# The order inside a group of expert matmuls: gate and up in turn, token tiles in turn

## The reference, cut to what matters

```
x = x + xattn(ctx, layernorm(x))          # scores, top 76 of each row, sigmoid, symmetrised
z = layernorm(x)
scores  = softmax(z @ gate_w.T);  weights, idx = top_k(scores, 2)
h   = einsum('td,eid->eti', z, w1)        # gate half, 128 hidden units per expert
g   = silu(h) * einsum('td,eid->eti', z, w3)   # times the up half
eo  = einsum('eti,edi->etd', g, w2)       # second projection
y   = sum over experts of eo * its weight (0 where not chosen)
out = x + y + shared expert of z (ws1, ws3, ws2)
```

## Time and profile before

| | before |
|---|---|
| median of 3 runs | 122.41 us |
| profiled execution | 122.40 us |
| its span | 120.6 us |
| TensorE busy (matmuls) | 105.2 us, 87% |
| VectorE busy | 83.1 us, 69% |
| GpSimd busy | 84.3 us, 70% |
| ScalarE busy | 55.0 us, 46% |
| mean granted TensorE clock | 0.929 of full speed |

### The profile page before, as it was taken

One profiled execution on the slowest core, in us unless ns is written; L12 is line 12 of the kernel. 1 busy time (PEld: TensorE's weight loads), 2 busy tenths in 40 slices (PEclk: granted clock), 3 DMA queues, 4 the chain that ended last, 5 costly groups with the idle time before them and its releaser, 6 DMA issues.

```text
span 120.6 us, 2390 instructions
## 1 busy us (share of the span) xinstructions
PE 105.2 (87%) x790; PEld 101.4 (84%) x790; DVE 83.1 (69%) x265; ACT 55.0 (46%) x128; POOL 84.3 (70%) x137
## 2 busy tenths in 40 slices
PE   6996082259999999999999999999989999999991
PEld 6775072158899989999999999999979999999990
DVE  6578996984695998769939896965555770708632
ACT  4149989299708612361768412104093243224310
POOL 4037878895799988999998899962827675075800
PEclk9999855555899999999999999999999999999999
DMA  2899992000000017000045000020441100902002
GB/s 55 206 297 297 323 369 79 0 5 3 0 5 0 0 44 313 0 3 0 0 130 226 0 0 0 8 90 0 163 185 43 49 0 3 345 8 90 0 0 87
DMA packets 7069, 10.32 MB, mean 86 GB/s; under 512 B 1360, under 2 KB 5968, under 8 KB 6544
## 3 DMA queue, kind: packets, MB, share of 16 engines
q1 hardware_dynamic: 6688, 10.13, 24.9%
q10 hardware_dynamic: 368, 0.04, 0.2%
HBM read 9.09 MB, written 1.08 MB: 84 GB/s over the span
## 4 chain that ended last, share of the span: by engine, by line
PE 75%; DVE 8%; ACT 5%; POOL 4%; issue 3%; DMA 2%; DVEq 1%; ACTq 0%; POOLq 0%; SPq 0%
PE ps_h L1248 21%; PE ps_u L1248 20%; PE ps_y L1276 16%; PE ps_u L1141 4%; PE ps_a L1276 3%; PE ps_c L1216 3%; PE ps_a L1176 2%; DMA weights<-gates 2%; PE ps_b L1199 2%; PE ps_h L1165 1%; DVE left L849 1%; POOL gc L423 1%; DVE near L855 1%; ACT qkT L551 1%; DVE g_lo L1001 1%
## 5 line engine op out<-in xcount | busy, mean ns | idle before, releaser
L423 POOL TENSOR_TENSOR gc<-prod,weights 128x512 f32<-128x512 f32 x16 | 25.5, 1609 | 13.3 <-DMA weights<-gates 7.4
L634 ACT ACTIVATE sil<-ps_h 128x512 f32<-128x512 f32 (+1 forms) x20 | 10.8, 549 | 25.1 <-PE ps_h L1248 24.8
L1001 DVE TENSOR_TENSOR g_lo<-gc,g_hi 128x512 fp32r<-128x512 f32 x16 | 13.3, 841 | 11.4 <-ACT g_hi L645 11.2
L1276 PE MATMUL ps_y<-dn_hi,g_hi 128*128 128x256 f32 x63 | 18.2, 289 | 0.5 <-DVE g_lo L1001 0.5
L1276 PE MATMUL ps_y<-dn_lo,g_hi 128*128 128x256 f32 x63 | 17.8, 282 | 0.0
L1276 PE MATMUL ps_y<-dn_hi,g_lo 128*128 128x256 f32 x63 | 17.8, 282 | 0.0
L645 ACT ACTIVATE g_hi<-gc 128x512 fp32r<-128x512 f32 x16 | 9.7, 625 | 13.8 <-POOL gc L423 13.8
L1248 PE MATMUL ps_h<-z_hi,up_hi 128*128 128x256 f32 x72 | 15.0, 289 | 0.3 <-issue 0.3
L1248 PE MATMUL ps_h<-z_lo,up_hi 128*128 128x256 f32 x72 | 14.5, 282 | 0.0
L1248 PE MATMUL ps_h<-z_hi,up_lo 128*128 128x256 f32 x72 | 14.4, 281 | 0.0
L1248 PE MATMUL ps_u<-z_hi,up_hi 128*128 128x256 f32 x72 | 14.4, 281 | 0.0
(11 more groups left out here) (173 smaller groups left out, 253.0 us busy)
## 6 DMA issues: line engine op xcount, KB each, us to landing
weights<-gates SPq DMA_DIRECT2D x4, 1024.0 KB, 4.5
x_sb<-in_x SPq DMA_DIRECT2D x4, 256.0 KB, 5.9
up_raw<-in_w1t SPq DMA_DIRECT2D x4, 256.0 KB, 6.4
up_raw<-in_w3t SPq DMA_DIRECT2D x4, 256.0 KB, 6.6
dn_raw<-in_w2t SPq DMA_DIRECT2D x4, 256.0 KB, 7.2
out_x<-fin SPq DMA_DIRECT2D x3, 256.0 KB, 2.4
out_x<-fin SPq DMA_DIRECT2D x2, 128.0 KB, 1.7
ctx_sb<-in_ctxT SPq DMA_DIRECT2D x1, 192.0 KB, 4.4
```

Of the source, the lines that this page charges most:

```text
L423: nc.gpsimd.tensor_tensor(gc[k % 2][:, :].rearrange("p (n t q) -> p n t q", n=2, t=T), prod[s][:, :].rearrange("p (n t q) -> p n t q", n=2 ...
L634: nc.scalar.activation(sil[i % 2][:, :w], ps_h[i % 2][:, :w], ACT.Silu).then_inc(silu_ready, 1)
L1001: nc.vector.tensor_tensor(g_lo[s][:, :], src[:, :], g_hi[s][:, :].bitcast(F32), ALU.subtract).then_inc(glo0_ready if s == 0 else glo_ready, 1)
L1276: last = nc.tensor.matmul(dst[:, t * D:(t + 1) * D], g[s][:, tok], w[:, e, :], start=(s == 0 and first and m == 0), stop=(s == SLOTS - 1 a ...
```

## The change

Two loops are written in another order. In the first projection the loop over the halves (a: gate, up) was the outermost; now it is the innermost, so a gate matmul into `ps_h` and an up matmul into `ps_u` alternate, both with the same moving operand. In the second projection the loop over the two token tiles moves inside the one over the three products; `down_last` keeps its order. `h_ready` is given by the last gate matmul and `u_ready` by the last up matmul, as before, and these are now the last two of the group. The waits for converted weights are for both halves at the start of a batch 0 group. The numbers of instructions are the same.

```
-                for a, (bank, ready) in enumerate(((ps_h, h_ready), (ps_u, u_ready))):
-                    for n, e in enumerate(experts_of(s)):
-                        dst = bank[i % 2][:, n * N:(n + 1) * N]
-                        m = 0
-                        for w, zz in ((up_hi, z_hi), (up_lo, z_hi), (up_hi, z_lo)):
-                            if b == 0 and n == 0 and m == 0:
-                                pe.wait_ge(up_hi_ready, 2 * s + a + 1)
-                            if b == 0 and n == 0 and w is up_lo:
-                                pe.wait_ge(up_lo_ready, 2 * s + a + 1)
-                            if zz is z_lo and a == 0 and n == 0:
-                                pe.wait_ge(zlo_ready, b + 1)
-                            for k in range(KD):
-                                last = nc.tensor.matmul(dst, w[:, e, a, k, :], zz[b % 2][:, k, :], ...)
-                                m += 1
-                    last.then_inc(ready, 1)
+                for n, e in enumerate(experts_of(s)):
+                    m = 0
+                    for w, zz in ((up_hi, z_hi), (up_lo, z_hi), (up_hi, z_lo)):
+                        if b == 0 and n == 0 and m == 0:
+                            pe.wait_ge(up_hi_ready, 2 * s + 2)
+                        if b == 0 and n == 0 and w is up_lo:
+                            pe.wait_ge(up_lo_ready, 2 * s + 2)
+                        if zz is z_lo and n == 0:
+                            pe.wait_ge(zlo_ready, b + 1)
+                        for k in range(KD):
+                            for a, bank in enumerate((ps_h, ps_u)):
+                                last = nc.tensor.matmul(bank[i % 2][:, n * N:(n + 1) * N], w[:, e, a, k, :],
+                                                        zz[b % 2][:, k, :], start=(m == 0), stop=(m == 3 * KD - 1))
+                                if m == 3 * KD - 1 and n == len(experts_of(s)) - 1:
+                                    last.then_inc((h_ready, u_ready)[a], 1)
+                            m += 1
...
             def down(b, s):
                 down_wait(b, s)
                 for n, e in enumerate(experts_of(s)):
-                    for t in range(T):
-                        last = down_tile(b, s, n, e, t)
+                    for m in range(3):
+                        for t in range(T):
+                            last = down_part(b, s, n, e, t, m)
                 last.then_inc(down_done, 1)
```

More of the change, by code:

```diff
@@ L1235, in up @@
                     pe.wait_ge(prod_ready, i - 1)
-                for a, (bank, ready) in enumerate(((ps_h, h_ready), (ps_u, u_ready))):
-                    for n, e in enumerate(experts_of(s)):
-                        dst = bank[i % 2][:, n * N:(n + 1) * N]
-                        m = 0
-                        for w, zz in ((up_hi, z_hi), (up_lo, z_hi), (up_hi, z_lo)):
-                            if b == 0 and n == 0 and m == 0:
-                                pe.wait_ge(up_hi_ready, 2 * s + a + 1)
-                            if b == 0 and n == 0 and w is up_lo:
-                                pe.wait_ge(up_lo_ready, 2 * s + a + 1)
-                            if zz is z_lo and a == 0 and n == 0:
-                                pe.wait_ge(zlo_ready, b + 1)
-                            for k in range(KD):
-                                last = nc.tensor.matmul(dst, w[:, e, a, k, :], zz[b % 2][:, k, :],
-                                                        start=(m == 0), stop=(m == 3 * KD - 1))
-                                m += 1
-                    last.then_inc(ready, 1)
+                for n, e in enumerate(experts_of(s)):
[14 more added lines that the diff above has]
+                            m += 1
             def down_wait(b, s):
@@ L1268, in down_wait, with down_part @@
                     pe.wait_ge(glo_ready, gated(b, s))
-            def down_tile(b, s, n, e, t):
+            def down_part(b, s, n, e, t, m):
+                g, w = ((g_hi, dn_hi), (g_hi, dn_lo), (g_lo, dn_hi))[m]
                 tok = slice(n * N + t * P, n * N + (t + 1) * P)
[L1273 to L1279, removed]
+                dst = ps_a if b == LAST and t == 1 else ps_y
+                first = t == 0 or b == LAST
+                return nc.tensor.matmul(dst[:, t * D:(t + 1) * D], g[s][:, tok], w[:, e, :],
+                                        start=(s == 0 and first and m == 0),
+                                        stop=(s == SLOTS - 1 and n == 1 and m == 2), skip_group_check=True)
             def down(b, s):
@@ L1291, in down_last @@
                     for n, e in enumerate(experts_of(SLOTS - 1)):
-                        last = down_tile(LAST, SLOTS - 1, n, e, t)
+                        for m in range(3):
+                            last = down_part(LAST, SLOTS - 1, n, e, t, m)
                     last.then_inc(last_tile, 1)
```

## The result

The changed kernel took 123.04 us as the median of 4 runs (122.80 to 123.64), the kernel before 122.03 us beside it (4 runs, 121.19 to 122.43). The ratio is 1.0124, with a 95% interval of 1.0071 to 1.0176: slower. The ratio is worked out from the single runs and is not the quotient of the two medians, which differ by 1.01 us, or 0.8%. The ratios in this document leave out executions in a slower state, two of the twelve of the second projection alone and two of the kernel before. The forecast was 123.5 us, with a range of 122.3 to 125.2.

A forecast was written before the change was run, and what follows sets the result against it. From about 31 us TensorE bounds the kernel, through its matmul count, step and waits. The terms 1.30 - 0.15 - 0.27 + 0.25 = +1.13 us on 122.40 us gave 123.5 us, range 122.3 to 125.2 us.

The forecast's parts named there:

- The step: Distance between matmuls in both projections: claimed unchanged at 0.118 to 0.120 us, term 0, bounds plus and minus 5 ns.
- the step rivals: Alternation shortens the distance between matmuls (5 ns: 120.3 us, chance 0.09) or lengthens it (5 ns: 126.8 us, chance 0.10).
- The wait for z: TensorE's transposes of batch 1's z wait behind the later silu of batch 0, slot 1: +1.30 us, down to 1.0.
- The wait for z_lo: Very first group, third product: wanted four matmuls later, so its weight load's wait shrinks: -0.15 us, between 0 and -0.19.
- The old wait at (0,3): Batch 0, slot 3, at 43.18 us: TensorE's wait for slot 1's product vanishes: -0.27 us, 0 the other end.
- The products that follow: VectorE's products come about 0.48 us later, behind silu; TensorE waits at batch 1, slot 3: +0.25 us, between 0 and 0.5.
- The remaining slots have more room: Slots after batch 1, slot 3: no added wait; the wait at 89.70 us moves as a whole.
- the tail: Last slot's g_lo and its matmuls: 0.83 us of slack against 0.48, so 0, at most 0.1 us.
- hidden after all: Rival: something after 38 us swallows the stall; with z in time, only 0.25 us left, 122.0 to 122.9 us; chance 0.13.
- The clock did not fall in the new wait: Rival: TensorE's clock falls in the new idle stretch around the transposes, 2.7 us lost, 126.2 us; chance 0.04.

The follow-up runs named there:

- the second projection alone: Only the second projection alternates its token tiles, first projection as in the kernel before; ratio to the kernel before 0.9995.
- the kernel with `ps_u` first: The kernel before with the halves swapped, all of ps_u filled and then all of ps_h, no alternation; ratio to the kernel before 1.0175.
- the first projection alone: Only the first projection alternates gate and up, second projection as in the kernel before; median 123.12 us, ratio to the kernel before 1.0128.
- z and product moved ahead: Changed kernel with batch 1's normalisation ahead of the silu of batch 0, slot 1, and that slot's product ahead of routing; ratio to the kernel before 1.0034.
- all but (0,1): The changed kernel, but with the gate and up group of batch 0, slot 1 in the old order; ratio to the kernel before 1.0062.
- z ahead: The changed kernel with batch 1's normalisation moved ahead of the silu of batch 0, slot 1 on ScalarE; median 122.82 us, ratio to the kernel before 1.0101.
- the two swaps and no alternation: Kernel before with batch 1's normalisation ahead of the silu of batch 0, slot 1, and that slot's product ahead of routing; ratio to the kernel before 0.9981.

## Why the prediction was right, point by point

**The step: 0, right.** It stayed at 0.117 to 0.120 us in every kernel. The bound of 5 ns from one change of bank was cautious; the kernel with `ps_u` first and the one with the second projection alone show that both signs of the step rivals were empty. The page "TensorE: Matmul & The Clock Gate" of the Trainium skill (section "Back-to-back issue gap") gives N/2.4 + 2.5 ns, an estimate of 109 ns, as the gap of a single isolated matmul, and sets a stream of weight loads and matmuls, as there is here, apart from it. So it was no measure of what alternation could win; the trace shows 117 to 120 ns with and without alternation, and the order of banks is not what separates the two.

**The wait for z: +1.30, measured +1.27 us.** The silu came 1.27 us later against its group, the two normalisations behind it, TensorE waited 1.15 us ahead of the transposes, and from start to start the whole delay arrived. The kernel that changes (0,1) alone confirms that it is this place.

**The wait for z_lo: -0.15, measured -0.26 us.** Right in sign and mechanism. The idle time of 0.19 us of a weight load was the wrong measure of what it cost: before, the matmul at 32.47 us came 0.27 us behind the one ahead of it and the next 0.22 us behind that, where steps of 0.12 stand now.

**The old wait at (0,3): -0.27, measured -0.41 us.** The mechanism held, with other instructions than said. The text had the second routing instruction find GpSimd free. In the trace it was still blocked. The product was ready 11.65 us after the start of the first group, 0.32 us later than before (11.33), but TensorE came to (0,3) 0.60 us later (12.03 against 11.43), without a wait:

```profile
40.13 0.46 DVE L970 TENSOR_TENSOR exc<-ex,chosen 128x16 f32<-128x16 f32 x1
...
40.70 1.14 DVE L975 TENSOR_TENSOR comb<-exc,exr 128x16 f32<-128x16 f32 x1
41.76 0.67 DVE L989 TENSOR_TENSOR prod<-sil,ps_u 128x512 f32<-128x512 f32 x1
```

```profile
39.09 2.72 POOL L312 TENSOR_TENSOR up_lo<-up_raw,up_hi 128x512 fp32r<-128x512 f32 x2
...
44.06 1.29 POOL L312 TENSOR_TENSOR up_lo<-up_raw,up_hi 128x512 fp32r<-128x512 f32 x1
```

The pair runs to 41.81 us, the second routing instruction to 41.84 us, and the product is ready at 42.43 us, 0.38 us before TensorE needs it. Again the wait was worth more than the idle time that its row gives (0.41 against 0.27 us; the reason stands in the last section).

**Not foreseen: +0.44 us ahead of (0,4).** The second up_lo row above is the cause. One more small routing instruction, of 0.18 us in the trace of before, ran into it, and the product of (0,2) behind it was late:

```profile
44.19 1.20 DVE L963 TENSOR_TENSOR chosen<-lgx,rest 128x16 f32<-128x16 f32 x1
45.41 0.69 DVE L989 TENSOR_TENSOR prod<-sil,ps_u 128x512 f32<-128x512 f32 x1
```

That product is ready at 46.10 us, and group (0,4) starts at 46.20. No run moves this product by itself. The prediction had delayed VectorE by 1.15 us ahead of (0,3) and looked only at what lay under GpSimd's first pair. It did not ask what the same delay pushes the next routing instructions into. The kernel with the first projection alone and the one with (0,1) alone show the same wait (0.31 and 0.25 us); the one with `ps_u` first does not.

**Not priced: the wait for both halves' weights.** The edit makes a batch 0 group wait for the low weights of both halves at its fifth matmul. The prediction gave this no term. In the changed kernel it cost nothing, since TensorE came to (0,4) at 46.20 us and the last up_lo was ready at 45.35. That was luck: in the two kernels where TensorE came earlier (z and product moved ahead, and all but (0,1)) the same wait cost 0.47 and 0.41 us.

**The products that follow: +0.25, measured -0.11 us.** VectorE's products did come to wait for ScalarE, as said, but the delay did not reach TensorE at (1,3):

```profile
49.81 0.69 DVE L989 TENSOR_TENSOR prod<-sil,ps_u 128x512 f32<-128x512 f32 x1 [0.98 <-ACT sil L634]
...
54.44 1.28 DVE L1001 TENSOR_TENSOR g_lo<-gc,g_hi 128x512 fp32r<-128x512 f32 x2
55.64 0.68 DVE L989 TENSOR_TENSOR prod<-sil,ps_u 128x512 f32<-128x512 f32 x1
```

The instructions of g_lo took less than before (the one of 1.78 us in the earlier trace rows), and the product was ready at 56.32 us, 0.7 us early: the lower end of the term's range. That it depends on where VectorE's instruction falls against GpSimd's fits these rows, but no run isolates it. With z ahead, and in the kernel of all but (0,1), where TensorE comes to (1,3) sooner, the wait is there, 0.39 and 0.38 us, and names the product.

**"The remaining slots have more room", 0: wrong by 0.44 us.** The transposes of z of batch 2 waited 0.23 us for ScalarE at 63.18 us. This is not the pattern of 38 us, for here ScalarE itself waited for GpSimd's scales, and no silu stood directly ahead:

```profile
62.04 1.09 ACT L618 ACTIVATE z<-x,nb,rs 128x256 f32<-128x256 f32 x2 [1.47 <-POOL nb L407]
```

The kernel with the two swaps and no alternation waits 0.19 us at the same place. So what the alternation has to do with it stays open. And the tail, given 0 to 0.1 us, cost 0.18:

```profile
112.30 0.69 DVE L989 TENSOR_TENSOR prod<-sil,ps_u 128x512 f32<-128x512 f32 x1 [0.82 <-ACT sil L634]
...
113.59 2.44 DVE L1001 TENSOR_TENSOR g_lo<-gc,g_hi 128x512 fp32r<-128x512 f32 x2 [0.60 <-ACT g_hi L645]
```

The g_lo before the last is the late one, not the last, for which the slack had been worked out.

**The rival "hidden after all"** fell in its condition. It said that with z in time only 0.25 us would be left. With z ahead of the silu 0.93 us of B were left, 1.14 us of the medians (122.82 against 121.68), for the reason shown above. The clock did not fall in the new wait: the strip shows full speed from the slice in which it rose to the end.

**Sum.** 1.13 us forecast, 1.37 us in the trace, 1.01 us between the medians (1.5 us by the ratio). The big term was right to 0.03 us. The others missed by 0.11 to 0.44 us each, with both signs, and partly cancelled. The forecast of 123.5 us also stood on 122.4 us for the kernel before, whose median in the 31 executions beside the last four kernels was 121.60; what can be compared is the difference.

## What to carry to other kernels

Before reordering a producer's work, ask for each consumer which of its inputs is complete later, and what stands behind it in that engine's own list: a delay in the middle of a queue is paid by the instruction behind, here a normalisation that had nothing to do with the experts. And before pricing a wait as the gain of removing it, look for the next limit at the same place: a swap that removed 1.15 us of waiting won 0.3 us of the medians until the second limit, a product behind small instructions behind another engine's large ones, was moved as well. Ask also when each input is first wanted: interleaving two halves makes the group want the second half's weights near its start. To see a delay of a microsecond in two traces, compare from the first instruction that the edit can reach, and start to start.

## What the runs showed of the hardware that was not expected

- A wait costs more than the idle time in its row. The 0.27 us of the earlier trace rows were worth 0.41 us, the 0.30 us ahead of (0,4) cost 0.44. This comes from how the rows are counted: idle time begins where the row of the matmul before ends, and that row is longer than a step. Ahead of (0,4) the matmul at 45.63 us has a row of 0.28 us, while without a wait the next would start after 0.12; it started after 0.57, which is 0.45 too late. Start to start gives the cost, the idle time does not.
- VectorE's instructions of 128x16 take 0.17 us, or up to 1.25 us if they start beside one of GpSimd's instructions of 1.27 us. A shift of a quarter of a microsecond decides which. The Trainium skill, "SBUF — State Buffer", section "Who interferes with whom", describes such a port held whole by one side; the rows agree, down to the second routing instruction of the changed kernel that ends within 0.03 us of GpSimd's pair.
- When the clock returns to full speed before the first group differs between executions of one kernel (about 29.0 us in the profile after, about 31.0 before). Of 31 executions of the kernel before, the 10 with a mean clock of 0.943 took 121.36 us on average and the other 21 took 121.71, so this explains a part of the spread of 120.76 to 122.17 us, not all of it. Of the 27 executions of the kernel before that stood beside four other kernels, the 10 at 0.943 took 120.98 us on average and the other 17 took 121.83. So the median of a few runs also depends on how many of them fell on each side.
